# First mixture of experts: results scattered to their tokens' rows, a deeper fetch, and routing work moved between engines

## The chip, the core and the metric

One Trainium2 chip, one core of it. The metric is device time in microseconds (us) for one execution of the whole program, lower is better. The figure of a kernel is the median of its timed runs. The rows below come from one profiled execution.

## What is computed

The program is two transformer-like layers on 4096 tokens (B = 4, a 32 x 32 grid) of C = 192 float32 channels: attention, a mixture of 8 experts, attention, then a second block with its own attention, feed-forward and mixture of 4. The change touches the first mixture alone:

```python
logits = jnp.einsum('btd,ed->bte', x, gate_w)            # x: normed tokens, 8 experts
probs = jax.nn.softmax(logits, axis=-1)
selected_probs, selected_idx = jax.lax.top_k(probs, 2)
selected_probs = selected_probs / (jnp.sum(selected_probs, axis=-1, keepdims=True) + 1e-08)
a = jnp.einsum('btd,edh->bteh', x, gate_bank)            # h = 384
u = jnp.einsum('btd,edh->bteh', x, up_bank)
h = jax.nn.silu(a) * u
y_all = jnp.einsum('bteh,ehd->bted', h, down_bank)
y = sum over the 2 selected experts of y_all * selected_probs
```

The result y is added to the residual.

## The kernel before, in words

`routed_experts` computes only the two chosen experts of each token. Each engine has an instruction list of its own in one block, and semaphores written by hand order them. Its stages are these.

**Norm and transposes.** VectorE (DVE) normalises 32 tiles of 128 tokens into `rows` (L1904; shown as y). TensorE (PE) transposes them in 8 chunks of 512 tokens (L1729, L1730), ScalarE (ACT) copies each chunk out of PSUM into `room` (L1834; shown as xt). SyncE (SP) stores the normed rows to the DRAM tensor `xn` (normed_rows). Beside this the expert weights are loaded in 8 blocks by SP (`load_weights`, four raw buffers), and split into a float16 high part (ACT, `split_high`, L1824, L1825) and a low part (DVE, `split_low`, L1912, L1916). DVE has six of the eight low splits in its list ahead of the routing.

**Logits.** After each chunk of transposes PE makes the logits of the chunk before (`logit`, L1718): the 128 tokens of a tile are the weights and the 8 columns of `gw` move, so a chunk has 4 tiles x 2 halves of C, and each float32 product shows as two records.

**Routing.** DVE takes maximum, softmax, top 2 (L1927 to L1951), PE counts and ranks (L1740 to L1745), and DVE computes for each of the 2 x 4096 (token, choice) pairs a slot in a list that is sorted by expert and padded to blocks of 256 rows: 39 blocks, 78 groups of 128. To invert the list, one-hot matrices are built: `hi_hot` (L1976), `by_place` (L1980), `lo_hot` (L1981) by DVE and `by_pick` (L1683) by GpSimd (POOL); PE multiplies them (L1754, L1758) and DVE makes from the product `ids`, the pair held by each slot, and `take`, the token row to fetch. Between, DVE computes which expert owns a block (L1985 to L1990) and makes the last two low splits.

**Blocks.** For each of 39 blocks POOL fetches 256 rows of `xn` by two indirect DMAs (`fetch`, L1693), up to AHEAD = 3 blocks ahead; PE transposes them, makes gate and up products (L1782 to L1786) and the down products (L1799); ACT and DVE do silu, product and splits; ACT writes the result into `done` (L1862), two blocks behind; SP stores it to `yd` (expert_rows) in the order of the slots (L1668).

**Return.** When all 39 stores are in DRAM, POOL gathers the rows of every token tile with 64 indirect DMAs (L1705), 32 into `rows` and 32 into `wide` (vt); DVE, chunk by chunk of 512 tokens, adds them into the residual with their gate values (L2039, 8 of 128 x 192) and takes the statistics for the next norm (L2044, 4). Then the block ends, SP clears the mixture's semaphores (40 of them), and the next layer's norm begins (L123).

Of the kernel before, what the change touches and what calls it, by code (L numbers as in the profile page):

```python
# [24 lines left out]
T = B * L  # L25
# [61 lines left out]
def linker(engine, sem):  # L87

    count = [0]

    def link(ins):
        count[0] += 1
        ins.then_inc(sem, 1)
        engine.wait_ge(sem, count[0])

    return link

# [1450 lines left out]
def routed_experts(nc, name, res, rows, room, wide, stats, eps, ident, a, scratch, sent, experts, mt, w_gate, gate_bank,  # L1548
# [12 lines left out]
    AHEAD = 3  # L1561
# [6 lines left out]
    with Pool(nc, name) as m:  # L1568
# [6 lines left out]
        gw = [m.sb("gw0", experts), m.sb("gw1", experts, parts=C1)]  # L1575
# [14 lines left out]
        take, give = m.sb("take", SLOTS, U32), m.sb("give", PAIR, U32)  # L1590
# [10 lines left out]
        fetched = [room[1][:, at + u * 2 * C:at + (u + 1) * 2 * C] for u in range(AHEAD)]  # L1601
        done = [rows[:, at + u * 2 * C:at + (u + 1) * 2 * C] for u in range(AHEAD)]
# [9 lines left out]
        logits, ranks, counts, lists = banks[4:8]  # L1612
# [6 lines left out]
        s_turn, s_f32, s_lg = m.sem("turn"), m.sem("f32"), m.sem("logits")  # L1619
# [4 lines left out]
        s_sent = [m.sem(f"sent{r}") for r in range(AHEAD)]  # L1624
        s_add, s_bn = m.sem("add"), m.sem("bn")
        s_fetch, s_back = sent["fetch"], sent["back"]
# [10 lines left out]
        with nc.Block() as block:  # L1637
            @block.sync
            def _(sp):
# [25 lines left out]
                for b in range(BLOCKS):  # L1665
                    u = b % AHEAD
                    sp.wait_ge(s_y, b + 1)
                    sp.dma_start(yd[b * SPAN:(b + 1) * SPAN, :].rearrange("(j p) f -> p j f", p=P),  # L1668
                                 done[u].rearrange("p (j f) -> p j f", j=2)).then_inc(s_sent[u], 16)
                for r in range(AHEAD):  # L1670
                    sp.wait_ge(s_sent[r], 16 * len(range(r, BLOCKS, AHEAD)))

            @block.gpsimd
            def _(pool):
                for i, t in enumerate(bl):
                    pool.memset(t[C1:P, :], 0.0).then_inc(s_pad, 1)
                    pool.wait_ge(s_pad, i + 1)
                pool.memset(ones[:, :], 1.0).then_inc(s_pad, 1)

                pool.wait_ge(s_const, 48)  # L1680
                pool.wait_ge(s_xn, 16 * (T // CHUNK))
# [27 lines left out]

            @block.tensor  # L1710
            def _(pe):
# [11 lines left out]
                for n in range(T // CHUNK):  # L1723
# [8 lines left out]
                    if n:  # L1732
                        logit(n - 1)
# [84 lines left out]
            def _(act):  # L1818
# [11 lines left out]
                for n in range(T // CHUNK):  # L1830
# [4 lines left out]
                    if n % 2:  # L1835
                        split_high(n // 2)
# [413 lines left out]
```

## Time and profile before

| | us |
|---|---|
| median of 3 runs | 3374.49 |
| lowest and highest | 3373.45, 3380.55 |
| the profiled execution, its own time | 3370.78 |
| its span | 3368.9 |
| share of the span: PE, DVE, ACT, POOL busy | 82%, 72%, 55%, 13% |

The first mixture lies between about 797 and 1204 us of the span. In the rows below a time line gives start and duration in us, the engine, the source line, output and inputs by their names, a count, and in brackets how long the engine had been idle and what ended that. A q behind an engine's name is its queue of DMA issues.

### The profile page before, as it was taken

The page shows a single profiled execution, that of the slowest core. Times are in us where ns is not written, and L with a number is a line of the kernel's source. Part 1 is how long each engine was busy: PE and PEld are TensorE (multiplying, and loading weights), DVE is VectorE, ACT ScalarE, POOL GpSimd, SP SyncE. Part 2 cuts the span into 40 slices and gives each one's busy share as a digit, 9 for nine tenths or more (in the row PEclk, how much of TensorE's full clock was granted, in tenths as well). Part 3 has the DMA queues.
Part 4 walks back from the last instruction along what each step waited for, and adds up shares of the span by engine and source line. Part 5 has one row for each costly group of instructions (what it writes and reads, how often), then busy time and mean ns, then how long its engine had stood idle before and what let it go on. Part 6 is the DMA issues. An engine that isn't in the chain of part 4 may idle for free. (4 is left out here: it accounts for less than half of the span.)

```text
span 3368.9 us, 62705 instructions
## 1 busy us (share of the span) xinstructions
PE 2764.8 (82%) x18708; PEld 1277.7 (38%) x18708; DVE 2414.6 (72%) x4597; ACT 1860.7 (55%) x2592; POOL 435.2 (13%) x513
## 2 busy tenths in 40 slices
PE   5948999997499239589999956199999959599999
PEld 3612222226499126222222234022222236366666
DVE  6458999974766354579999955589999835465665
ACT  4416777773255124167777736067777736465554
POOL 0010111111333510101111110201111100000000
PEclk9759999996699667599999977599999979699999
DMA  2555776664122214567766701101111110200000
GB/s 64 169 125 114 151 148 142 148 126 143 33 78 76 70 31 146 134 110 150 149 146 149 145 22 50 57 28 52 48 48 49 48 32 1 55 22 5 9 5 14
DMA packets 202070, 277.27 MB, mean 82 GB/s; under 512 B 54302, under 2 KB 93454, under 8 KB 201930
## 3 DMA queue, kind: packets, MB, share of 16 engines
q1 hardware_dynamic: 162346, 211.32, 27.1%
q0 software_dynamic: 19920, 31.57, 4.0%
q10 hardware_dynamic: 19664, 32.60, 3.3%
q8 instruction: 77, 1.26, 0.2%
q14 instruction: 63, 0.52, 0.1%
HBM read 196.93 MB, written 77.46 MB: 81 GB/s over the span
## 5 line engine op out<-in xcount | busy, mean ns | idle before, releaser
L750 DVE TENSOR_REDUCE c1att_mx<-c1att_m 128x1 f32<-128x512 f32 x768 | 493.4, 685 | 35.7 <-PE c1att_m L688 30.6
L750 DVE TENSOR_REDUCE c0att_mx<-c0att_m 128x1 f32<-128x512 f32 x768 | 493.4, 685 | 32.5 <-PE c0att_m L688 27.2
L750 DVE TENSOR_REDUCE f1att_mx<-f1att_m 128x1 f32<-128x512 f32 x768 | 493.3, 685 | 26.5 <-PE f1att_m L688 21.8
L996 ACT ACTIVATE c1att_p<-c1att_s 128x1024 f32<-128x1024 f32 x384 | 373.9, 1020 | 152.0 <-PE c1att_s L703 151.9
L996 ACT ACTIVATE c0att_p<-c0att_s 128x1024 f32<-128x1024 f32 x384 | 373.9, 1020 | 148.8 <-PE c0att_s L703 148.7
L996 ACT ACTIVATE f1att_p<-f1att_s 128x1024 f32<-128x1024 f32 x384 | 373.9, 1020 | 143.8 <-PE f1att_s L703 142.8
L1426 ACT ACTIVATE moe_h<-moe_u,moe_bu 128x512 f32<-128x512 f32 x192 | 136.5, 711 | 175.6 <-PE moe_u L1343 93.9
L688 PE MATMUL f1att_m<-f1att_km,f1att_qm 16*128 16x512 f16 x768 | 155.7, 401 | 88.6 <-DVE f1att_ka L959 52.9
L716 PE MATMUL f1att_o<-f1att_p,f1att_vs 128*32 128x512 f32 x1536 | 206.2, 609 | 0.6 <-ACT f1att_p L996 0.6
L716 PE MATMUL c0att_o<-c0att_p,c0att_vs 128*32 128x512 f32 x1536 | 206.2, 609 | 0.6 <-ACT c0att_p L996 0.6
L716 PE MATMUL c1att_o<-c1att_p,c1att_vs 128*32 128x512 f32 x1536 | 206.1, 609 | 0.6 <-ACT c1att_p L996 0.6
L688 PE MATMUL c1att_m<-c1att_km,c1att_qm 64*128 64x512 f16 x768 | 156.2, 402 | 58.0 <-DVE c1att_mx L750 35.0
L688 PE MATMUL c0att_m<-c0att_km,c0att_qm 64*128 64x512 f16 x768 | 156.3, 403 | 57.7 <-DVE c0att_mx L750 34.8
L703 PE MATMUL f1att_s<-f1att_qa,f1att_ka 113*128 113x512 f16 x768 | 202.7, 385 | 0.8 <-ACT f1att_p L996 0.4
L1356 PE MATMUL moe_y<-moe_dh,xt 128*128 128x192 f16 x1536 | 195.1, 246 | 0.0
L1463 DVE TENSOR_TENSOR xt<-moe_h,xt 128x512 f16<-128x512 f32 x192 | 131.3, 691 | 86.3 <-ACT xt L1428 85.3
L1356 PE MATMUL moe_y<-moe_dl,xt 128*128 128x192 f16 x768 | 188.9, 246 | 0.0
L688 PEld LDWEIGHTS f1att_m<-f1att_km,f1att_qm 16*128 16x128 f16 x768 | 37.3, 92 | 322.6 <-DVE f1att_mx L750 264.3
L688 PEld LDWEIGHTS c1att_m<-c1att_km,c1att_qm 64*128 64x128 f16 x768 | 37.8, 93 | 292.3 <-DVE c1att_mx L750 262.4
L688 PEld LDWEIGHTS c0att_m<-c0att_km,c0att_qm 64*128 64x128 f16 x768 | 37.8, 93 | 291.7 <-DVE c0att_mx L750 262.2
L703 PE MATMUL c1att_s<-xt,c1att_ka 113*128 113x512 f16 x512 | 135.7, 387 | 7.6 <-DMA xt<-c1att_mrow 7.1
L1356 PEld LDWEIGHTS moe_y<-moe_dh,xt 128*128 128x128 f16 x1536 | 139.0, 98 | 3.7
(608 smaller groups left out, 5430.8 us busy)
## 6 DMA issues: line engine op xcount, KB each, us to landing
xt<-rel_parts SPq DMA_DIRECT2D x256, 128.0 KB, 5.0
xt<-qk_parts SPq DMA_DIRECT2D x192, 128.0 KB, 4.4
y<-rel_parts SPq DMA_DIRECT2D x128, 128.0 KB, 5.6
y<-qk_parts SPq DMA_DIRECT2D x96, 128.0 KB, 5.1
c0att_qm<-rel_parts SPq DMA_DIRECT2D x144, 64.0 KB, 2.1
c1att_qm<-rel_parts SPq DMA_DIRECT2D x144, 64.0 KB, 2.1
expert_rows<-y SPq DMA_DIRECT2D x39, 192.0 KB, 2.0
o_sums<-c0att_o ACTq DMA_DIRECT2D x24, 256.0 KB, 4.3
```

Of the source, the lines that this page charges most:

```text
L688: ins = pe.matmul(bank[:, :], qm[v][rows, q0:q0 + P], km[v][rows, c * CHUNK:(c + 1) * CHUNK], start=True, stop=True)
L703: ins = pe.matmul(sps[h][:, c * CHUNK:(c + 1) * CHUNK], ka[u][0:R_END, kcol], qa[u][0:R_END, queries(h, version, c * CHUNK, CHUNK)], start ...
L716: ins = pe.matmul(ops[row:row + 32, :], vs[u][:, (h * KT + kt) * 32:(h * KT + kt + 1) * 32], pr[h][kt % 2][:, c * CHUNK:(c + 1) * CHUNK], ...
L750: dve.tensor_reduce(mx[:, n:n + 1], bank[:, :], AX.X, ALU.max).then_inc(s_mx, 1)
L996: act.activation(pr[h][kt % 2][:, :], sps[h][:, :], ACT.Exp).then_inc(s_e, 1)
L1356: ins = pe.matmul(yps[q % 2][t // 2][:, (t % 2) * C:(t % 2 + 1) * C], hidden[q % 2][:, x], down[:, w], start=k == 0 and i == 0, stop=k == ...
L1426: act.activation(h32[:, i % 2 * CHUNK:(i % 2 + 1) * CHUNK], bank[:, :], ACT.Gelu, bias=bias, scale=1.0 / W_SCALE).then_inc(s_h32, 1)
L1463: dve.tensor_tensor(hl[q % 2][:, cols], h32[:, i * CHUNK:(i + 1) * CHUNK], hh[q % 2][:, cols], ALU.subtract).then_inc(s_hl, 1)
```

## The change

- **Return.** `send(b)` on POOL writes each block's 256 result rows by two indirect DMAs straight to row "choice x 4096 + token" of `yd`; the places are `give` (now from `ids`, one for each slot; empty slots are out of bounds and skipped). When all are there, SP reads `yd` back in order with 16 plain DMAs. The 39 stores by SP and the 64 gathers by POOL are gone.
- **Fetch.** Rows are fetched 6 blocks ahead, results kept in 3 buffers. POOL's list: six fetches, then `send(b)` and `fetch(b + 6)` in turn.
- **Logits.** `gw` is padded to 32 columns (two memsets by POOL ahead of its others, and SP waits for them before its first load) and is now the weights; 512 tokens move. Four chunks use the four 32-column tiles of PE side by side, twice. ACT copies the product out, PE transposes it back, DVE copies it from PSUM in 8 pieces. The splits of blocks 2 and 3 by ACT come after the last logits instead of among the chunks.
- **One-hot products.** `by_pick` is made by DVE; its order is `hi_hot`, `lo_hot`, `by_place`, `by_pick`.
- `s_back` (8 semaphores) and two for the logits are now among those cleared at the end, three fewer `s_sent`: 47.

```diff
-    AHEAD = 3
+    AHEAD, KEPT = 6, 3
...
-        gw = [m.sb("gw0", experts), m.sb("gw1", experts, parts=C1)]
+        gw = [m.sb("gw0", 32), m.sb("gw1", 32, parts=C1)]
...
-        take, give = m.sb("take", SLOTS, U32), m.sb("give", PAIR, U32)
+        take, give = m.sb("take", SLOTS, U32), m.sb("give", SLOTS, U32)
...
             def _(sp):
...
+                sp.wait_ge(s_pad, 2)
                 for t, src in zip(gw, (w_gate[0:C0, :], w_gate[C0:C, :])):
-                    sp.dma_start(t[:, :], src).then_inc(s_gw, 16)
+                    sp.dma_start(t[:, 0:experts], src).then_inc(s_gw, 16)
...
-                for b in range(BLOCKS):
-                    u = b % AHEAD
-                    sp.wait_ge(s_y, b + 1)
-                    sp.dma_start(yd[b * SPAN:(b + 1) * SPAN, :].rearrange("(j p) f -> p j f", p=P),
-                                 done[u].rearrange("p (j f) -> p j f", j=2)).then_inc(s_sent[u], 16)
-                for r in range(AHEAD):
-                    sp.wait_ge(s_sent[r], 16 * len(range(r, BLOCKS, AHEAD)))
+                for r in range(KEPT):
+                    sp.wait_ge(s_sent[r], 32 * len(range(r, BLOCKS, KEPT)))
+                for n in range(T // CHUNK):
+                    for k, tile in enumerate((rows, wide)):
+                        src = yd[k * T + n * CHUNK:k * T + (n + 1) * CHUNK, :]
+                        sp.dma_start(tile[:, n * 4 * C:(n + 1) * 4 * C].rearrange("p (t f) -> p t f", t=4),
+                                     src.rearrange("(t p) f -> p t f", p=P)).then_inc(s_back[n], 16)
...
             def _(pool):
+                for t in gw:
+                    pool.memset(t[:, :], 0.0).then_inc(s_pad, 1)
...
-                pool.wait_ge(s_hot, 2)
-                pool.tensor_tensor(by_pick.rearrange("p (k s) -> p k s", s=SLOTS),
-                                   hi_hot.rearrange("p (k s) -> p k s", s=SLOTS),
-                                   table[:, COUNT:COUNT + PAIR].unsqueeze(2).broadcast_to([P, PAIR, SLOTS]),
-                                   ALU.mult).then_inc(s_picks, 1)
...
+                def send(b):
+                    u = b % KEPT
+                    pool.wait_ge(s_y, b + 1)
+                    for j in range(2):
+                        pool.indirect_dma_start(
+                            yd[:, :], bass.IndirectOffsetOnAxis(give[:, 2 * b + j:2 * b + j + 1], 0),
+                            done[u][:, j * C:(j + 1) * C], None,
+                            bounds_check=2 * T - 1, oob_is_err=False).then_inc(s_sent[u], 16)
+
+                pool.wait_ge(s_xn, 16 * (T // CHUNK))
                 pool.wait_ge(s_idx, 2)
+                for b in range(AHEAD):
+                    fetch(b)
                 for b in range(BLOCKS):
-                    fetch(b)
-                for r in range(AHEAD):
-                    pool.wait_ge(s_sent[r], 16 * len(range(r, BLOCKS, AHEAD)))
-                for n in range(T // CHUNK):
-                    for k, tile in enumerate((rows, wide)):
-                        for t in range(4 * n, 4 * n + 4):
-                            pool.indirect_dma_start(
-                                tile[:, t * C:(t + 1) * C], None, yd[:, :],
-                                bass.IndirectOffsetOnAxis(give[:, k * TILES + t:k * TILES + t + 1], 0)
-                                ).then_inc(s_back[n], 16)
+                    send(b)
+                    if b + AHEAD < BLOCKS:
+                        fetch(b + AHEAD)
...
-                def logit(n):
-                    pe.wait_ge(s_f32, 2 * n + 2)
-                    for j in range(4):
-                        t = 4 * n + j
-                        for k, c in enumerate((C0, C1)):
-                            ins = pe.matmul(logits[:, t * experts:(t + 1) * experts], room[k][0:c, t * P:(t + 1) * P],
-                                            gw[k][0:c, :], start=k == 0, stop=k == 1)
+                def logits(i):
+                    pe.wait_ge(s_f32, 8 * i + 8)
+                    for k, c in enumerate((C0, C1)):
+                        for j in range(4):
+                            ins = pe.matmul(banks[4 + i][32 * j:32 * j + 32, :], gw[k][0:c, :],
+                                            room[k][0:c, (4 * i + j) * CHUNK:(4 * i + j + 1) * CHUNK],
+                                            start=k == 0, stop=k == 1)
                     ins.then_inc(s_lg, 1)
+
+                def logits_back(i):
+                    pe.wait_ge(s_lgc, i + 1)
+                    for t in range(4):
+                        ins = pe.transpose(banks[6 + i][:, t * P:(t + 1) * P], raw_lg[i][:, t * P:(t + 1) * P], ident)
+                    ins.then_inc(s_lgt, 1)
...
-                    if n:
-                        logit(n - 1)
-                logit(T // CHUNK - 1)
+                    if n == 4:
+                        logits(0)
+                    if n == 6:
+                        logits_back(0)
+                logits(1)
+                logits_back(1)
...
-                    if n % 2:
-                        split_high(n // 2)
-                for blk in range(T // CHUNK // 2, experts - 2):
+                    if n % 4 == 1:
+                        split_high(n // 4)
+                    if n == 4:
+                        logits_out(0)
+                logits_out(1)
+                for blk in range(2, experts - 2):
                     split_high(blk)
...
-                    if b >= AHEAD:
-                        act.wait_ge(s_sent[u], 16 * (b // AHEAD))
+                    if b >= KEPT:
+                        act.wait_ge(s_sent[u], 32 * (b // KEPT))
...
+                for i in range(2):
+                    dve.wait_ge(s_lgt, i + 1)
+                    to = key[:, i * 16 * experts:(i + 1) * 16 * experts].rearrange("p (j t e) -> p t j e", j=4, e=experts)
+                    source = banks[6 + i][:, :].rearrange("p (t j e) -> p t j e", t=4, j=4)
+                    for t in range(4):
+                        inc(dve.tensor_copy(to[:, t], source[:, t, :, 0:experts]))
+                link(dve.memset(low_one[:, 0:1], 0.0))
...
+                dve.wait_ge(s_hot, 2)
+                dve.tensor_scalar(by_place, hi_hot, place[:, :], None, ALU.mult).then_inc(s_hot, 1)
+                dve.wait_ge(s_xn, 16 * (T // CHUNK))
+                dve.tensor_tensor(by_pick.rearrange("p (k s) -> p k s", s=SLOTS),
+                                  hi_hot.rearrange("p (k s) -> p k s", s=SLOTS),
+                                  table[:, COUNT:COUNT + PAIR].unsqueeze(2).broadcast_to([P, PAIR, SLOTS]),
+                                  ALU.mult).then_inc(s_picks, 1)
...
-                dve.tensor_copy(give[:, :], slot[:, :]).then_inc(s_idx, 1)
+                link(dve.tensor_scalar(empty[:, :], ids[:, :], 0.0, 1.0e5, ALU.is_lt, ALU.mult))
+                dve.tensor_tensor(give[:, :], ids[:, :], empty[:, :], ALU.add).then_inc(s_idx, 1)
...
-                    dve.wait_ge(s_back[n], 128)
+                    dve.wait_ge(s_back[n], 32)
```

## Rows read from the trace of the kernel before

**Rows 1.** The page's first line: the span.
```profile
span 3368.9 us, 62705 instructions
```

**Rows 2.** Busy time by stretch: PE, PEld, DVE, ACT, POOL, then clock, DMA share, GB/s.
```profile
920.00:960.00 40.00, 40.00 (x404) 37.30 (x403) 24.63 (x64) 23.70 (x72) 14.36 (x16) 1.00 0.29 78
1130.00:1206.00 76.00, 0.00 (x0) 0.00 (x0) 29.00 (x89) 0.00 (x0) 51.95 (x53) 0.50 0.26 70
2924.60:2932.30 7.70, 7.61 (x33) 0.96 (x34) 0.00 (x0) 0.62 (x2) 0.00 (x0) 0.50 0.66 174
```

**Rows 3.** DVE in order of time, the return: first chunk, last chunk, next layer.
```profile
1127.36 1.40 DVE L2039 SCALAR_TENSOR_TENSOR x<-y,f_top,x 128x192 f32<-128x192 f32 x4 [16.68 <-DMA vt<-expert_rows,f_give]
...
1199.50 1.41 DVE L2039 SCALAR_TENSOR_TENSOR x<-y,f_top,x 128x192 f32<-128x192 f32 x4 [6.36 <-DMA vt<-expert_rows,f_give]
...
1202.38 1.14 DVE L2044 BATCH_NORM_STATS2 stats<-x 128x6 f32<-128x192 f32 x4
1206.99 0.21 DVE L123 TENSOR_TENSOR c1ln_mean<-stats 128x32 f32<-128x32 f32 x1 [3.47 <-PEq L68]
```

**Rows 4.** POOL in order of time: the last of the 64 gathers.
```profile
1196.84 0.94 POOL L1705 DMA_INDIRECT vt<-expert_rows,f_give  x1 [0.30 <-issue]
```

**Rows 5.** ACT in order of time: results of blocks 0, 36 and 38.
```profile
921.79 0.48 ACT L1862 ACTIVATE y<-f_bank 128x384 f32<-128x384 f32 x1
...
1108.43 0.48 ACT L1862 ACTIVATE y<-f_bank 128x384 f32<-128x384 f32 x1
...
1112.58 0.49 ACT L1862 ACTIVATE y<-f_bank 128x384 f32<-128x384 f32 x1 [1.67 <-PE f_bank L1799]
```

**Rows 6.** Program start: SP's loads of x, 768 KB each, and DVE's first work on them.
```profile
0.99 4.92 SPq L2124 DMA_DIRECT2D x<-in_x  x4
```
```profile
5.96 2.18 DVE L2119 BATCH_NORM_STATS2 stats<-x 128x6 f32<-128x192 f32 x8 [5.96 <-DMA x<-in_x]
```

**Rows 7.** Groups of POOL instructions: busy us, mean ns, idle before them and releasers.
```profile
L1693 POOL DMA_INDIRECT xt<-normed_rows,f_take x78 | 73.8, 947 | 120.4 <-PE f_bank L1769 99.8 <-issue 12.8 <-DVE f_give L2001 7.8
```

**Rows 8.** PE in order of time: the last logits here, and the second mixture's.
```profile
841.19 8.28 PE L1718 MATMUL f_bank<-f_gw,xt 128*128 128x8 f32 x32
```
```profile
2924.69 7.52 PE L1102 MATMUL moe_y<-xt,moe_gw 128*32 128x512 f32 x32 [16.86 <-DMA moe_b<-in_exp_b]
2932.14 1.97 PE L1109 MATMUL moe_y<-ident,moe_h 128*128 128x128 f32 x8
```

**Rows 9.** ACT and SP in order of time: high splits of blocks 4 and 5, block 5's load.
```profile
844.62 0.51 ACT L1824 ACTIVATE f_ah<-vt 128x384 f16<-128x384 f32 x1
...
848.50 0.67 ACT L1825 ACTIVATE f_dh<-vt 128x576 f16<-128x576 f32 x1
```
```profile
834.56 0.59 SPq L1648 DMA_DIRECT2D vt<-in_f_down  x1
```

**Rows 10.** DVE in order of time: first routing step, then one-hots to the index list.
```profile
852.39 0.41 DVE L1927 TENSOR_REDUCE f_one<-f_bank 128x32 f32<-128x256 f32 x1
...
869.52 5.36 DVE L1976 TENSOR_TENSOR xt<-f_table,f_slothi 128x4992 f16<-128x4992 f32 x1
...
876.36 8.68 DVE L1981 TENSOR_TENSOR vt<-f_table,f_slotlo 128x8192 f16<-128x8192 f32 x1
884.96 8.83 DVE L1985 TENSOR_TENSOR f_past<-f_table,f_ends 128x312 f32<-128x312 f32 x1
...
894.43 0.55 DVE L1912 SCALAR_TENSOR_TENSOR f_al<-f_raw,f_ah 128x384 f16<-128x384 f32 x1
...
899.51 0.22 DVE L1995 TENSOR_SCALAR f_ids<-f_bank 128x78 f32<-128x78 f32 x1
```

**Rows 11.** POOL in order of time: its first memsets, `by_pick`, the first fetch.
```profile
797.39 5.36 POOL L1676 MEMSET f_bl<- 64x3072 f16 x2 [10.60 <-POOLq L68]
...
876.62 16.83 POOL L1683 TENSOR_TENSOR y<-xt,f_table 128x4992 f16<-128x4992 f16 x1 [73.60 <-DVE xt L1980]
901.28 1.07 POOL L1693 DMA_INDIRECT xt<-normed_rows,f_take  x1 [7.83 <-DVE f_give L2001]
```

More of the change, by code:

```diff
@@ L96, in linker, with chain, inc, link @@
     return link
+def chain(engine, sem):
+    count = [0]
+    def inc(ins):
+        count[0] += 1
+        ins.then_inc(sem, 1)
+    def link(ins):
+        inc(ins)
+        engine.wait_ge(sem, count[0])
+    return link, inc
 def layer_norm(nc, name, src, eps, stats, turned_to, ident, gain=None, shift=None, parts=None, inner=None, direct=False):
@@ L1600, in routed_experts @@
         at = (PAIR * SLOTS + 1) // 2
-        fetched = [room[1][:, at + u * 2 * C:at + (u + 1) * 2 * C] for u in range(AHEAD)]
-        done = [rows[:, at + u * 2 * C:at + (u + 1) * 2 * C] for u in range(AHEAD)]
+        fetched = [rows[:, at + u * 2 * C:at + (u + 1) * 2 * C] for u in range(AHEAD)]
+        done = [room[1][:, at + u * 2 * C:at + (u + 1) * 2 * C] for u in range(KEPT)]
         at = PAIR * P
@@ L1611, in routed_experts @@
         t0, t1 = banks[0:2], banks[2:4]
-        logits, ranks, counts, lists = banks[4:8]
+        ranks, counts, lists = banks[4:7]
+        raw_lg = [wide[:, 2 * RAW + i * CHUNK:2 * RAW + (i + 1) * CHUNK] for i in range(2)]
         turned, units, sums = banks[0:2], banks[2:6], banks[6:8]
@@ L1618, in routed_experts @@
         s_chain, s_std, s_norm, s_xn = m.sem("chain"), m.sem("std"), m.sem("norm"), m.sem("xn")
-        s_turn, s_f32, s_lg = m.sem("turn"), m.sem("f32"), m.sem("logits")
+        s_turn, s_f32, s_lg, s_lgc, s_lgt = (m.sem(n) for n in ("turn", "f32", "logits", "lcopy", "lturned"))
         s_exp, s_route, s_chosen, s_rank = m.sem("exp"), m.sem("route"), m.sem("chosen"), m.sem("rank")
@@ L1623, in routed_experts @@
         s_up, s_s, s_h32, s_hh, s_hl, s_down, s_y = (m.sem(n) for n in ("up", "s", "h32", "hh", "hl", "down", "y"))
-        s_sent = [m.sem(f"sent{r}") for r in range(AHEAD)]
+        s_back = [m.sem(f"back{n}") for n in range(T // CHUNK)]
         s_add, s_bn = m.sem("add"), m.sem("bn")
-        s_fetch, s_back = sent["fetch"], sent["back"]
+        s_fetch, s_sent = sent["fetch"], sent["sent"]
         def cube(t):
@@ L1826, in split_high, with logits_out @@
                                    scale=W_SCALE).then_inc(s_wh, 1)
+                def logits_out(i):
+                    act.wait_ge(s_lg, i + 1)
+                    act.activation(raw_lg[i], banks[4 + i][:, :], ACT.Copy).then_inc(s_lgc, 1)
                 act.wait_ge(s_chain, 6)
@@ L1884, in _ @@
             def _(dve):
-                link = linker(dve, s_chain)
+                link, inc = chain(dve, s_chain)
                 half_of = stats[:, :].rearrange("p (t s) -> p s t", s=6)
@@ L1978, in _ @@
                                   slot_hi[:, :].unsqueeze(2).broadcast_to([P, PAIR, SLOTS]), ALU.is_equal).then_inc(s_hot, 1)
-                dve.wait_ge(s_hot, 1)
-                dve.tensor_scalar(by_place, hi_hot, place[:, :], None, ALU.mult).then_inc(s_hot, 1)
                 dve.tensor_tensor(lo_hot.rearrange("p (k s) -> p k s", s=P),
@@ L2106, in build @@
         by_pool = {"past": 0} | {k: ctx.enter_context(nc.semaphore(f"{k}_by_pool")) for k in ("z", "rzst", "numinv")}
-        sent = {k: [ctx.enter_context(nc.semaphore(f"{k}{r}_by_pool")) for r in range(n)] for k, n in (("fetch", 3), ("back", T // CHUNK))}
+        sent = {k: [ctx.enter_context(nc.semaphore(f"{k}{r}_by_pool")) for r in range(n)] for k, n in (("fetch", 6), ("sent", 3))}
         with Pool(nc, "start") as m:
```

18 lines of the change are left out of this document (7 added, 11 removed).

## The prediction

> **What bounds the kernel now.** The change touches one stage, so I read the page for the span [rows 1] and then only that stage, first as busy time by stretch, then each engine in order of time. Three regimes are to be seen. In the block loop PE is busy 40.00 us of 40.00 at full clock [rows 2]: nothing in the loop that is not PE can save time, it can only cost some. In the return PE is at 0.00, DVE is busy 29 of 76 us and the DMA engines are at 0.26 of their time, while POOL is at work throughout [rows 2]: POOL's descriptor work sets the pace. DVE waited 16.68 us for its first chunk and 6.36 us before its last [rows 3], and the gathers follow each other at 0.94 + 0.30 us, started by nothing but the end of the one before [rows 4]. Between norm and loop there is a serial chain: the last logits, the routing, the one-hots, the index list, the first fetch [rows 8, 10, 11].
>
> **Return, the large term.** Before: the last result is in SBUF at 1112.58 + 0.49 = 1113.07 [rows 5], the last statistics end at 1202.38 + 1.14 = 1203.52 [rows 3]; 90.45 us. After, in the times of this trace: POOL must still send blocks 36, 37 and 38, the first and last of whose results come at 1108.43 + 0.48 = 1108.91 and 1113.07 [rows 5], closer together than two sends a block would be. A scatter does not occur before. Nearest is the gather: 1.25 us from one to the next [rows 4], of which 0.947 us work [rows 7]. I take 1.25 us. Six in a row from 1109.1 put the last issue at 1115.35. From issue to the released reader the last gather took 1199.50 - 1196.84 = 2.66 us [rows 3, 4], so the rows are in DRAM at 1118.0. SP then reads 768 KB for each chunk of 512 tokens, as much as one load of x at the start has; the first of these took 5.96 - 0.99 = 4.97 us until DVE began, and four were issued in 4.92 us [rows 6]. DVE begins at 1123.0. A chunk is 1202.38 + 1.14 - 1199.50 = 4.02 us of DVE work [rows 3]; the x loads were issued at 1.23 us for 768 KB, so even two DMAs for each chunk at that price, 2.5 us, stay ahead, and DVE sets the pace: 8 x 4.02 and 0.05 between them is 32.5, end 1155.5. Gain 48.0 us. If the first chunk lands after 4 or 8 us it is 49 or 45.
>
> **The loop.** Removed: 39 issues on SP, which costs nothing, as SP has nothing else there. Added: 78 scatters in POOL's list, in front of each later fetch. The deeper fetch gives nothing, since PE never idled between 920 and 960 [rows 2] with three ahead. It is cover: with six ahead, a fetch queued behind a send that waits for its result is still in time. POOL's sum: the first send can start at 922.27 [rows 5], and behind it are 66 fetches and 78 sends. With 1.25 us each they end no earlier than 922.27 + 180 = 1102.3, and the last result is at 1113.07; so they fit, with 11 us to spare in 191. That slack is thin: a scatter of 1.42 us uses it up, and each further 0.1 us costs 7.8 us at the end. ACT waits for the send of three blocks ago before it writes `done`: nothing until POOL is that far behind. The memory traffic is the same as before.
>
> **One-hots.** From `hi_hot` to the first fetch it is now 901.28 - 869.52 = 31.76 us [rows 10, 11]. The chain ran through POOL: `by_pick` ends at 876.62 + 16.83 = 893.45 [rows 11], then PE's second half, then DVE's index work at 899.51. DVE was held too: `past`, 312 columns, took 8.83 us and ended as POOL did [rows 10], where 4992 columns took 5.36. After, on DVE alone: `hi_hot` and `by_place` 6.84 (876.36 - 869.52), `lo_hot` 8.60, `by_pick` unknown, `past` some 0.5, its two followers 0.6, the two low splits 899.51 - 894.43 = 5.08, the index work to the first fetch 1.77, `give` in two steps +0.27. For `by_pick` the same number of columns and the same table as operand as in `hi_hot` say 5.36; bounds are 1.5 (the whole difference 6.84 - 5.36, for `by_place`) and 8.8. The sum is 29.0; gain 2.7 us (6.5 to -0.7). PE's first half lies under `by_pick`, the second under the splits, which last longer.
>
> **Logits.** Old: 16 records in 4.1 us, after each chunk (8.28 us for the last 32 [rows 8]), 33 us in all with PE the pace, the last at 849.5. New, from the second mixture, which has this very form: 32 records in 7.52 us and the transposes back in 1.97, at the low clock 0.50 [rows 2, 8]. So PE gets some 24 us back. But DVE and ACT take over: DVE's list has six low splits ahead of the routing, ACT now has splits 2 to 5 behind `logits_out(1)`. With transposes at some 1.7 us for a chunk and ACT's two copies and splits between, I get the last logits at about 830, and ACT's four splits at (848.50 + 0.57 - 844.62) / 2 = 2.2 us each [rows 9] from 830.6. Block 5's weights are issued at 834.56 [rows 9], at the end of one unbroken series on SP, and land by 834.56 + 4.97 = 839.5 at the latest by the bound of [rows 6]. So high part 5 ends at 841.7, low part 5 (5.08 / 2 = 2.54) at 844.25, the eight small copies and the memset 1.2 more (0.9 to 2.2: 0.24 each is the pitch of a small DVE instruction that waits [rows 3], and these don't wait), and the two new memsets in front of everything 0.3. Routing starts at 845.75 instead of 852.39: gain 6.6 us (3 to 8.5). The routing itself doesn't change.
>
> **Block end.** 40 semaphores are cleared within 3.47 us [rows 3], at most 0.09 each; seven more, 0.5 us.
>
> **Sum.** -48.0 - 2.7 - 6.6 + 0.5 = -56.8 us. The profiled execution took 3370.78 us, 3.7 below the median 3374.49, so it would give 3314; on the median 3317.7. I predict 3318.
>
> **A rule that speaks against it.** The stores leave SP for POOL, and POOL's work can be held up by DVE: `past` and `by_pick` above hindered each other [rows 10, 11]. In the loop, though, fetches cost 0.947 us in the mean beside a DVE that is busy 24.63 of 40 us [rows 2, 7]. The Trainium skill, "SBUF — State Buffer", section "Who interferes with whom", says that DMAs issued by GpSimd starve while VectorE runs an operation that takes both ports, and advises SP or ACT as issuer. By that rule each scatter might wait for a DVE instruction; by the rows none does.
>
> **Rivals.**
> - *POOL becomes the bound of the loop.* For: a slack of 0.17 us for each scatter; bounds checking and DRAM as the target have no row. Against: 0.947 on all 78 fetches. If a scatter waited for one DVE instruction of some 0.4 us (1.67), POOL ends at 922.27 + 82.5 + 130.3 = 1135, not 1116.6: +18.5, 3336.
> - *The front gives nothing*: weights land later or the splits are the true chain. For: six low splits stand before the routing. Against: block 5 is issued by 835. Time 3374.5 - 47.5 = 3327.
> - *The read back is not faster than the gathers*, 10.4 us for a chunk (1.3 x 8), because it is the rows of 768 bytes and not the descriptors that cost. For: as many rows. Against: DMA share 0.26 then [rows 2]. Gain some 9 + 9: 3356.
> - *Slower*: a scatter costs 2.2 us or more, 1.75 times a gather. Then POOL ends at 922.27 + 82.5 + 171.6 = 1176, +60, and PE waits in the loop for its fetches: 3377 and more. It decides from 2.17 us on.
>
> **Chances.** The forecast 0.66 (own range 3309 to 3325), POOL as bound 0.17 (3320 to 3345), front nothing 0.08, slow read back 0.05, slower 0.04. The range takes in the first three: 3305 to 3336. A measurement of this kernel tells about 0.2%, 7 us, from no change. Faster 0.95, same 0.01, slower 0.04.
>
> **What would show it.** The last result to the next norm in about 42 + 4 us; scatters at 1.25 us pitch; PE without idle time in the loop; DVE's return chunks back to back; routing 6 to 7 us earlier, bounded by low part 5; `by_pick` near 5.4 us and `past` near 0.5. I would be wrong if the scatters' pitch is over 1.42, if DVE waits before each chunk of the return, or if the clock falls in the loop.

## The result, and the profile after

The kernel after took 3402.57 us (median of four runs, 3399.93 to 3406.23), the kernel before, timed beside it, 3375.21 us; the ratio is 1.0079 [1.0062, 1.0097]. So the change came out slower by 0.8%, where the prediction said 3318 us. Later the same file, unchanged, was loaded anew four times in three other jobs and took 3315 to 3317 us each time, 1.6% faster than the kernel before. (A job is one stay on a chip, in which several kernels are timed in turn, the kernel before always among them.) Both numbers have to be explained, and only one of them is.

First the profile of that first timing, which I call the first job. The page's span, and its granted clock in 40 slices of the span, in tenths of full speed:

```profile
span 3402.8 us, 62616 instructions
...
PEclk9759999997688858579999987599999979699999
```

Busy time by stretch: the start of the loop, the rest of the loop, the return (columns as in [rows 2]):

```profile
905.00:920.00 15.00, 12.46 (x103) 9.88 (x101) 6.70 (x18) 6.07 (x21) 4.06 (x5) 0.93 0.13 36
920.00:1185.00 265.00, 223.68 (x1872) 184.21 (x1871) 111.68 (x288) 102.46 (x322) 139.58 (x138) 0.88 0.18 50
1190.00:1230.00 40.00, 0.00 (x0) 0.00 (x0) 28.80 (x89) 0.17 (x1) 3.64 (x4) 0.55 0.52 158
```

In the loop PE is busy 84% of the time, where it was busy 40.00 of 40 us [rows 2], and its granted clock is 0.88 in place of 1.00. Half of the 83 us that the loop lost, as worked out below, is PE's idle time, 41.3 us between 920 and 1185; the rest is time in which PE counts as busy and gets on more slowly, its matmuls at the lower clock above all. The groups of waits in the loop (us in total, times, the longest) name hardly any engine and no DMA for PE:

```profile
DVE vt L2066 <- ACT vt L1904: 115.3, 50, 8.1
POOL expert_rows L1713 <- ACT xt L1895: 100.2, 26, 11.3
...
PEld f_bank L1809 <- issue: 13.5, 13, 1.4
PEld f_bank L1812 <- issue: 12.7, 13, 1.3
PEld f_bank L1825 <- issue: 9.8, 11, 1.9
```

"issue" means that the profile shows nothing for which the engine waited. The named waits of PE in this stretch come to 5.0 us, six waits for DVE's `xt`. POOL waits for results (100.2 us), so it is not the bound: it waits for the others. PE in order of time, inside such a gap:

```profile
958.27 0.27 PE L1810 MATMUL f_bank<-vt,f_ah 128*128 128x256 f16 x1
958.54 0.27 PE L1811 MATMUL f_bank<-vt,f_bh 128*128 128x256 f16 x1
959.28 0.27 PE L1812 MATMUL f_bank<-vt,f_bl 128*128 128x256 f16 x1 [0.47 <-issue]
960.01 0.27 PE L1808 MATMUL f_bank<-vt,f_ah 128*128 128x256 f16 x1 [0.46 <-issue]
960.72 0.27 PE L1809 MATMUL f_bank<-vt,f_al 128*128 128x256 f16 x1 [0.44 <-issue]
960.83 0.27 PE L1810 MATMUL f_bank<-vt,f_ah 128*128 128x256 f16 x1
962.14 0.38 PE L1811 MATMUL f_bank<-vt,f_bh 128*128 128x256 f16 x1 [1.04 <-issue]
962.32 0.42 PE L1812 MATMUL f_bank<-vt,f_bl 128*128 128x256 f16 x1
```

The profile shows nothing that they wait for; they start every 0.72 us, or after twice that, instead of every 0.11 us. The matmul at 962.14 takes 0.38 us and the next 0.42, in place of 0.27: the clock has gone from 2.4 to 1.2 GHz behind the gap, as the clock column (the third from the right) says of the gap and of the time behind it:

```profile
958.50:961.00 2.50, 1.14 (x6) 0.23 (x4) 0.00 (x0) 0.00 (x0) 1.99 (x2) 1.00 0.23 79
962.20:964.00 1.80, 1.28 (x5) 0.50 (x6) 0.00 (x0) 0.14 (x1) 0.04 (x1) 0.50 0.21 55
```

POOL meanwhile issues at its usual pitch:

```profile
957.34 1.03 POOL L1713 DMA_INDIRECT expert_rows<-xt,f_give  x1 [0.30 <-issue]
958.68 1.00 POOL L1713 DMA_INDIRECT expert_rows<-xt,f_give  x1 [0.30 <-issue]
959.99 0.98 POOL L1705 DMA_INDIRECT y<-normed_rows,f_take  x1 [0.30 <-issue]
```

Such gaps come in a pattern that for most of the loop repeats every 22.7 us, three blocks: when POOL issues eight DMAs in one go, PE stalls for some 5 us in the second half of them and 1.2 us beyond; four in one go leave one short gap of 0.2 to 1.6 us or none, and the longer of these are put down to DVE's `xt`. Three blocks take 22.7 us in place of 15.6. PE's gaps without a named wait, those over 0.2 us, all start 4.8 us or more behind the first DMA of such a go and end within 2 us of its last.

Outside the loop the stage is near the forecast. DVE and ACT in order of time, from the last result to the next layer:

```profile
1189.68 0.49 ACT L1895 ACTIVATE xt<-f_bank 128x384 f32<-128x384 f32 x1 [1.93 <-issue]
...
1200.34 1.41 DVE L2082 SCALAR_TENSOR_TENSOR x<-y,f_top,x 128x192 f32<-128x192 f32 x4 [12.51 <-DMA vt<-expert_rows]
...
1231.11 1.14 DVE L2087 BATCH_NORM_STATS2 stats<-x 128x6 f32<-128x192 f32 x4
1235.62 0.22 DVE L138 TENSOR_TENSOR c1ln_mean<-stats 128x32 f32<-128x32 f32 x1 [3.37 <-PEq L68]
```

The return is 1190.17 to 1232.25, 42.1 us, where it was 90.45 (worked out from [rows 3, 5]). POOL's first memset starts at 801.63 (797.39 in [rows 11]), the routing at 848.70, the first fetch at 895.40 and the last result ends at 1190.17. Against [rows 3, 5, 10, 11] the stage's parts are: up to the routing -7.9 us, routing to first fetch -2.2, loop +83.0, return -48.4, block end -0.1; in sum +24.4. The loop's 294.8 us (211.8 before) hold the whole miss.

### The profile page after: what moved, and what is told of

Its sections match the earlier page's. It is cut to its first block and busy times, and to the rows that moved or that the text cites. A ratio compares the mean times of both kernels' runs of the same rounds, so it can differ in the third digit from the quotient of the medians.

```text
span 3402.8 us, 62616 instructions
## 1 busy us (share of the span) xinstructions
PE 2782.0 (82%) x18620; PEld 1259.2 (37%) x18620; DVE 2413.9 (71%) x4608; ACT 1857.8 (55%) x2594; POOL 439.1 (13%) x528
## 5 line engine op out<-in xcount | busy, mean ns | idle before, releaser
L2066 DVE SCALAR_TENSOR_TENSOR vt<-f_bank,vt 128x256 f32<-128x256 f32 x117 | 49.7, 425 | 161.3 <-ACT vt L1904 127.0
```

What stands on the lines that cost most here:

```text
L2066: dve.scalar_tensor_tensor(out=h32[n % 2], in0=units[n % UNITS][:, SPAN:2 * SPAN], scalar=1.0 / W_SCALE, in1=s_buf[n % 2], op0=ALU.mult, o ...
```

## The experiments

I took the sends for the cause, since the stalls came when POOL issued without a break. The first four kernels ran together, in another job (the kernel before: 3369.68 us there). The first two leave out that the results reach their tokens' rows.

**plain_stores**, no sends: SP stores results in slot order and nothing gathers them.

```
-                for b in range(BLOCKS):
-                    send(b)
-                    if b + AHEAD < BLOCKS:
-                        fetch(b + AHEAD)
+                for b in range(AHEAD, BLOCKS):
+                    fetch(b)
...
+                    sp.dma_start(yd[b * SPAN:(b + 1) * SPAN, :].rearrange("(j p) f -> p j f", p=P),
+                                 done[u].rearrange("p (j f) -> p j f", j=2)).then_inc(s_sent[u], 16)
```

> Everything of the change but the scatters: SP stores each block's result in slot order as the kernel before did, POOL only fetches (six ahead), and the return reads the first 8192 slots in order, so the rows added are not those of their tokens. Theory 1 (POOL's indirect DMAs, four for a block and nearly without a gap, hold up PE's instruction stream): no gaps in PE's stream, loop back to 5.2 us a block, time about 3318. Theory 2 (the scatters' writes to DRAM): the same here. Theory 3 (the six-deep fetch or the new places of the buffers in SBUF): the loop stays at about 7.5 us a block, time about 3400.

Measured: 3309.85 us, ratio 0.982 [0.980, 0.984], no stall: as theories 1 and 2 had it.

**twins**, two more gathers in each pair of sends' place, SP storing:

```
+                        pool.indirect_dma_start(
+                            dump[u][:, j * C:(j + 1) * C], None, xn[:, :],
+                            bass.IndirectOffsetOnAxis(take[:, 2 * b + j:2 * b + j + 1], 0)).then_inc(s_twin[u], 16)
```

> As plain_stores, and POOL makes two further gathers for each block into unused SBUF, at the place in its list where the scatters stood. Same number of indirect DMAs as the changed kernel, but no scatter. Theory 1: the same gaps in PE's stream (5 us long, from some 6 us after the start of a run of eight), about 7.5 us a block, time 3395 to 3405. Theory 2: no gaps, about 3320. Theory 3: as plain_stores.

Measured: 3320.04 us, 0.985 [0.9831, 0.987], as theory 2 had it. POOL issued 122 gathers in a row with no more than 0.5 us between two (0.44 ahead of each block's added pair, 0.30 otherwise), and PE did not stall.

**ahead4**, `AHEAD, KEPT = 4, 3`:

> The changed kernel with rows fetched four blocks ahead and not six; POOL's opening run is eight fetches and not twelve. Theories 1 and 2: the same time within 5 us (3395 to 3405), since each block still has four indirect DMAs. Theory 3, if the depth is the cause: faster by tens of us.

Measured: 3617.82 us, 1.0734 [1.0712, 1.0755], which none of the three theories had. The waits between 940 and 1170 us are of another kind than the first job's:

```profile
POOL expert_rows L1713 <- ACT xt L1895: 149.2, 17, 9.3
PEld f_bank L1794 <- DMA y<-normed_rows,f_take: 107.5, 17, 7.2
PE f_bank L1794 <- DMA y<-normed_rows,f_take: 103.7, 17, 6.9
```

PE's transposes wait for a fetch, once a block, 6 us. The fetch of block b + 4 stands in POOL's list behind the two sends of block b, which wait for b's result, and PE needs it in block b + 3. So depth is needed for this order of the list, for a reason that has nothing to do with the first job's stalls.

**front_only**, the new logits and one-hots with the loop and the return of before (AHEAD = 3, SP's stores, POOL's 64 gathers):

> The new logits, the one-hot products all by VectorE and the padded gate weights, but loop and return as before. My working for the front alone: 9.3 us gained less nothing at the end of the block, so 3366 against 3375 (ratio 0.9972); the trace of the changed kernel has the first fetch 10.1 us earlier after the start of the stage, which would give 3365. Rival: the front's gain is lost again in the loop, ratio 1.000.

Measured: 3362.91 us, 0.9978 [0.9969, 0.9988], or -7.4 us (-10.5 to -4.0). In its trace the stage, from POOL's first memset to the next layer's first work, is 10.0 us shorter.

By then I believed in the sends (theory 2). The next four asked which property of them it was (the kernel before: 3370.82 us).

**no_check** gives each empty slot a spare row behind the 8192 (three more lines for DVE, not shown), so that the bound falls away:

```
-                            done[u][:, j * C:(j + 1) * C], None,
-                            bounds_check=2 * T - 1, oob_is_err=False).then_inc(s_sent[u], 16)
+                            done[u][:, j * C:(j + 1) * C], None).then_inc(s_sent[u], 16)
```

> The kernel after, with the sends' test of the row number taken away: every empty slot gets a spare row of its own behind the 8,192 (two more small operations by VectorE ahead of the loop), so that nothing has to be left out and no send carries a bound; the sent rows of tokens and their order are the same. Theory A (it is the bounds test: the two register moves of 0.58 us ahead of each pair of sends, and what the test does on GpSimd while TensorE issues in steps of 0.7 us): the stalls of 5 us in every third block go, the loop is 5.2 us a block again, some 3,312 to 3,322 us. Theory B (it is the sends themselves, DMAs by row numbers that write DRAM from SBUF): the pairs of moves go but TensorE stalls as before, 3,395 to 3,405 us.

**in_order** drops the bound too and sends each block's rows to neighbouring places, which are not their tokens':

```
+                link(dve.tensor_scalar(token[:, :], table[:, COUNT:COUNT + SLOTS], float(P), place[:, :], ALU.mult, ALU.add))
+                dve.tensor_scalar(give[:, :], token[:, :], -1.0, None, ALU.add).then_inc(s_idx, 1)
```

> As no_check, but the sends' row numbers are 128 s + p, the slots' own order, so that each send writes 128 rows side by side (its result is not the tokens': the return reads the first 8,192 slots). Theory B1 (sends write rows that lie all over DRAM, and that is what holds TensorE): 3,312 to 3,322 us if no_check is slow. Theory B2 (any send by row numbers): as no_check, within 0.3%. If no_check is fast this is fast too.

**twins_check** puts `bounds_check=T - 1, oob_is_err=False` on the two added gathers of twins:

> twins (rows stored in slot order by SyncE, two more gathers of each block in the sends' place) with the bounds test on those two gathers, so that GpSimd makes the same two register moves ahead of them as the kernel after makes ahead of its sends. Theory A (bounds test): TensorE stalls in steps of 0.7 us again and the time is above 3,380 us. Theory B (sends): as twins, 3,320 us within 0.3%.

**sp_late** adds `sp.wait_ge(s_y, BLOCKS)` ahead of SP's waits on the sends:

> The kernel after, but SyncE waits for the last block's result before it looks at the sends' semaphores; in the kernel after it stands on the first of them through the whole loop. Theory C (TensorE's slow issue comes from an engine that stands waiting on a semaphore that GpSimd's DMAs raise): the stalls go, 3,312 to 3,322 us. Theories A and B: no change, 3,400 us within 0.3%.

Measured: no_check 3317.92 us (0.9846 [0.9829, 0.9864]), in_order 3315.44, twins_check 3318.41, sp_late 3316.62. All fast, none with a stall. Each theory has a run against it: sp_late keeps the bound and is fast, and so is twins_check (against A, the bounds test); no_check, in_order and sp_late keep the sends and are fast (against B); no_check keeps SP's early wait and is fast (against C). What the four share is that they are not the first job. That was the theory to test next, and it should have been the first.

**after_again**, the unchanged file, and **sp_twice**, which repeats SP's last wait so that its code is one instruction longer:

```
+                sp.wait_ge(s_xn, 16 * (T // CHUNK))
                 for r in range(KEPT):
```

> The kernel after, unchanged, run again. Theory C (SyncE's early wait on the sends' semaphores holds TensorE back): 3,400 us within 0.3%, with the stalls of 0.7 us a step in every third block, as in its first run. Theory D (the stalls are no property of the program: no_check left SyncE's wait as it was, sp_late left the sends' bounds test, twins_check put the test on gathers, and none of the three stalled, so what they have in common is only that they are not that build in that run): 3,312 to 3,322 us and no stall.

> The kernel after with one more SyncE wait, on the normed rows' semaphore that it has just waited for, so that it is met at once: SyncE still stands on the sends' semaphores through the loop, and only SyncE's code is one instruction longer, as in sp_late. Theory C: 3,400 us within 0.3%. Theory D, or a fourth (E: where the code lies decides, and one instruction moves it): 3,312 to 3,322 us. after_again tells D from E: by E it is slow, by D fast.

Measured: after_again 3316.01 us (four runs, 3307.99 to 3319.02), 0.9831 [0.981, 0.9853]; sp_twice 3313.61. The windows of after_again, start of the loop, loop, return:

```profile
905.00:920.00 15.00, 15.00 (x150) 13.89 (x148) 9.87 (x26) 8.91 (x29) 6.48 (x7) 1.00 0.16 45
920.00:1100.00 180.00, 180.00 (x1805) 167.83 (x1803) 107.65 (x278) 102.23 (x310) 133.91 (x135) 1.00 0.27 72
1105.00:1145.00 40.00, 0.00 (x0) 0.00 (x0) 29.40 (x91) 0.37 (x1) 3.55 (x4) 0.54 0.52 158
```

PE is busy 180.00 of 180 us at clock 1.00, with the same instructions, while POOL issues 101 DMAs without a break. The stalls are no fixed property of the program.

**after_third** and **ahead5** (`AHEAD, KEPT = 5, 3`):

> The kernel after, unchanged, a third time. Theory D (the stalls belong to the one execution job in which it was first timed): 3,316 us within 0.3%, ratio 0.982 to 0.985, no step of 0.7 us. If the stalls come back here, they belong to the program and some condition that differs from job to job, and the time is 3,400 us within 0.3%.

> The kernel after with AHEAD = 5 (ahead4 took 3,618 us, TensorE stood 6 us a block on a fetch that GpSimd had queued behind two sends). In ahead4's trace a fetch lands some 6.5 us after the result that lets its block's sends start, and the transposes that need it come one block of 5.2 us too early; one block more of depth gives 5.2 us. First theory (the queue behind the sends decides, and five blocks are enough): 3,316 us within 0.5%. Second theory (a block more is not quite enough, TensorE waits about 1 us a block): about 3,390 us. The prediction's own words (depth is cover and gives nothing) hold between five and six if the first is right.

Measured: after_third 3316.46 us, 0.9841 [0.9828, 0.9854], no stall. ahead5 3345.33 us, 0.9928 [0.991, 0.9946], between the two theories. Its waits from 920 to 1120:

```profile
POOL expert_rows L1713 <- ACT xt L1895: 28.4, 21, 2.8
PEld f_bank L1794 <- DMA y<-normed_rows,f_take: 26.0, 26, 2.5
PE f_bank L1794 <- DMA y<-normed_rows,f_take: 19.8, 24, 2.3
```

26 waits for a fetch of 1.0 us each: the same mechanism as in ahead4, nearly hidden.

**ahead8** (`AHEAD, KEPT = 8, 3`), **after_fourth** and **after_fifth** (unchanged):

> The kernel after with AHEAD = 8. From 4 to 5 to 6 blocks of depth the time fell 3,618, 3,345, 3,316 us. First theory (at six no fetch is waited for: TensorE is busy 40.00 of 40 us in the rerun of the kernel after): 3,316 us within 0.3%. Second (GpSimd's four DMAs a block fill its 5.2 us and it falls behind late in the loop, which more lead would hide): some 3 to 6 us less.

> The kernel after, unchanged, a fourth time. 3,316 us within 0.3% and no steps of 0.7 us if the first job's stalls stay alone; 3,400 us if they are a state that the program's loads fall into now and then.

> The same file once more, loaded anew. As after_fourth: 3,316 us within 0.3% without the stalls, or 3,400 us if they are a state of some loads.

Measured: ahead8 3319.21 us (0.9847 [0.983, 0.9864]), after_fourth 3316.74, after_fifth 3315.47. Two blocks more of depth give nothing, and the stalls don't come back.

**load_half** and **load_full** add useless traffic beside the loop, 512 and 2048 rows for each block:

```
+                for b in range(BLOCKS):
+                    sp.wait_ge(s_y, b + 1)
+                    sp.dma_start(scratch["spill"][b * SPILL:(b + 1) * SPILL, :], xn[0:SPILL, :]).then_inc(s_spill, 16)
```

> The kernel after, with useless traffic beside its loop: at each block's result SyncE starts a copy of 512 normed rows (393 KB) from DRAM to DRAM, which in some 5.2 us adds as much again as the loop's own 74 GB/s of reads. Theory F (the first job's stalls came from other traffic to memory or on the DMA engines in that job, and TensorE's instructions wait with the rest): steps of 0.7 us in TensorE's issue, with no wait for a fetch, and some 3,330 to 3,400 us. Against it (the traffic is not what did it): 3,316 to 3,325 us, or, if longer, TensorE waiting for fetches, which the first job's profile doesn't show.

> As load_half with 2,048 rows (1.57 MB) a block, more than the DMA engines can move in 5.2 us. TensorE will wait for late fetches here under either theory; what is asked is whether its trace also has the steps of 0.7 us in the issue of matmuls between waits (theory F) or only waits on fetches (against it). Time 3,450 to 3,800 us.

Measured: 3404.28 us (1.0085 [1.0065, 1.0105]) and 3411.33 us (1.0102 [1.0073, 1.0131]), both with the steps of 0.7 us. That looks like theory F. But load_full was expected at 3450 us or more with waits for fetches, and its trace has two such waits between 920 and 1185, 3.1 us in all; and the kernel before took 3375.88 us in this job. PE of load_full in order of time:

```profile
907.94 0.27 PE L1814 MATMUL f_bank<-vt,f_al 128*128 128x256 f16 x1
908.44 0.27 PE L1815 MATMUL f_bank<-vt,f_ah 128*128 128x256 f16 x1 [0.22 <-issue]
909.82 0.27 PE L1816 MATMUL f_bank<-vt,f_bh 128*128 128x256 f16 x1 [1.12 <-issue]
910.54 0.28 PE L1817 MATMUL f_bank<-vt,f_bl 128*128 128x256 f16 x1 [0.45 <-issue]
911.24 0.39 PE L1813 MATMUL f_bank<-vt,f_ah 128*128 128x256 f16 x1 [0.42 <-issue]
```

and SP's queue:

```profile
919.88 8.27 SPq L1685 DMA_DIRECT2D spilled_rows<-normed_rows  x2
```

The first stall, 907.9 to 911.2, lies ahead of the first copy at 919.88, so the copies can't have made it; nor have the sends, the first of which is issued at 920.6. It lies where the first job had one too (909.6 to 912.3), at the end of POOL's first twelve fetches. And 0.79 of the DMA engines' time and 259 GB/s in the loop (0.18 and 50 in the first job) left PE about as busy, 218.07 us of 265 (223.68). The columns are as in [rows 2]:

```profile
920.00:1185.00 265.00, 218.07 (x1846) 180.14 (x1844) 110.18 (x284) 101.62 (x317) 138.98 (x138) 0.90 0.79 259
```

From the first fetch to the last result the loop takes 293.5 us in load_half and 298.0 in load_full, against 294.8 in the first job. What load_full's time has more comes at the return too, where DVE first waits 21.25 us for its rows (12.75 in load_half).

**load_full_again**, the same file:

> load_full once more, the same file. Its job and the first job had one thing in common: the kernel before took 3,375.2 and 3,375.9 us in them, and 3,369.5 to 3,371.3 us in the five jobs without stalls. Theory G (the chip or its state decides, not the traffic: 23 MB and 58 MB moved in the same 230 us gave stalls of one kind, and the first of them came at 908 us, before the first copy): where the kernel before takes some 3,370 us this one shows no step of 0.7 us, and takes 3,316 to 3,340 us; where it takes some 3,375 us, 3,411 us and the stalls. Theory F (the traffic makes them): 3,411 us within 0.4% and the steps, whatever the kernel before takes.

Measured: 3409.8 us, 1.010 [1.0083, 1.0116], stalls again, the first from 904.9 to 907.7, and the first copy is issued at 916.4. Its loop takes 300.4 us. The kernel before took 3377.85 us. By its own condition this run is of the slower sort of job, where theories F and G say the same, so it does not tell them apart.

The jobs side by side, with the number of the chip that each ran on:

| job | chip | before, us | kernels of the change in it | TensorE's steps of 0.7 us |
|---|---|---|---|---|
| first | not on record | 3375.21 | after 3402.6 | yes |
| 2 | 14 | 3369.68 | plain_stores, twins, front_only; ahead4 waits for fetches | no |
| 3 | 14 | 3370.82 | no_check, in_order, twins_check, sp_late 3315 to 3318 | no |
| 4 | 15 | 3371.28 | after_again 3316.0, sp_twice 3313.6 | no |
| 5 | 14 | 3369.52 | after_third 3316.5, ahead5 | no |
| 6 | 13 | 3370.03 | after_fourth 3316.7, after_fifth 3315.5, ahead8 | no |
| 7 | 10 | 3375.88 | load_half 3404.3, load_full 3411.3 | yes |
| 8 | 6 | 3377.85 | load_full_again 3409.8 | yes |

The chips separate the jobs as well as anything does: none of the five jobs on chips 13, 14 and 15 stalled, and the two on chips 10 and 6 did. No chip is known to have had both, and the unchanged file is not known to have run on chip 10 or 6.

## Why the prediction was wrong

**The step that failed** is "The loop": removed and added work at nothing, and PE as the only bound. In the first job the loop took 83.0 us more. It did not fail by the condition that the prediction named. A send costs 1.01 to 1.04 us in the mean (1.31 to 1.34 from one to the next), under the 1.42 us from which POOL would become the bound, and POOL waited 100 us for results. (The prediction took 1.25 us. Its 11 us of slack over 78 sends allow 1.39 and not 1.42, which changes nothing here.) What replaced it: PE's own issue in steps of 0.72 us, each gap followed by the lower clock. "The clock falls in the loop" was on the list of what would make the forecast wrong; the rivals had no mechanism for it.

**What is shown of the cause.** The stalls are not fixed in the program: four later loads of the unchanged file show PE without idle time, two of them with four and five runs. They are no wait for a fetch: ahead4 and ahead5 show what that looks like. The kernel before has at most a little of them in the three stalled jobs: its medians lie within 0.3% of each other in all eight, so the condition of the job alone doesn't cost it what it costs the kernel after. The first stall of a loop needs neither a send nor a copy, as both come later.

**What stays open.** What the three stalled jobs had in common, and what in the kernel after answers to it and in the kernel before doesn't. The chip is a rival that no run tests: a property of chips 10 and 6 fits the table as well as a state that comes and goes. The kernel before was slower in just these three, by 4 to 8 us; that is a correlation over eight jobs, not a cause. Nor is it shown that the kernel before is free of stalls there. Its one trace has none: its first twelve fetches too follow without a break, from 901.28 to 916.24, and PE stays busy behind them, where the four stalled traces have their first stall.

```profile
915.00:920.00 5.00, 5.00 (x52) 4.68 (x51) 3.11 (x8) 2.50 (x8) 1.69 (x2) 1.00 0.17 43
```

But that execution took 3370.78 us, less than any of the first job's four timed runs (3373.45 and more) and as much as the median in jobs without stalls, so it doesn't stand for a stalled job. That the added traffic has no part in the later stalls of jobs 7 and 8 is likely, since four times as much moved the time by 0.2%, but it is not shown: the unchanged file ran in no second job of the slower sort. Also, plain_stores, twins, no_check, in_order, twins_check and sp_late all ran in jobs in which nothing stalled. Their speed says nothing on whether sends, bounds or POOL's long runs matter in a stalling job; the reading "it is the sends", which I drew from the first two, was wrong to draw. The next step would be one job on chip 10 or 6, and one on chip 14, each with the unchanged file, the kernel before and the file without its sends, all traced.

**The rest by its steps, in after_again**, where nothing stalled. The rows that answer to [rows 3, 5, 10, 11] follow, engine by engine in order of time. POOL at the stage's start:

```profile
800.02 0.17 POOL L1693 MEMSET f_gw<- 128x32 f32 x2 [10.50 <-POOLq L68]
```

ACT and DVE, block 5's first high split and last low one; DVE, the first routing step and the one-hots:

```profile
841.58 0.52 ACT L1850 ACTIVATE f_ah<-vt 128x384 f16<-128x384 f32 x1 [2.01 <-DMA vt<-in_f_down]
...
845.83 0.74 DVE L1949 SCALAR_TENSOR_TENSOR f_dl<-vt,f_dh 128x576 f16<-128x576 f32 x1
...
847.41 0.42 DVE L1965 TENSOR_REDUCE f_one<-f_key 128x32 f32<-128x256 f32 x1
...
864.13 5.36 DVE L2013 TENSOR_TENSOR xt<-f_table,f_slothi 128x4992 f16<-128x4992 f32 x1
869.40 8.68 DVE L2016 TENSOR_TENSOR vt<-f_table,f_slotlo 128x8192 f16<-128x8192 f32 x1
878.12 1.52 DVE L2020 TENSOR_SCALAR xt<-xt,f_place 128x4992 f16<-128x4992 f16 x1
879.56 5.35 DVE L2022 TENSOR_TENSOR y<-xt,f_table 128x4992 f16<-128x4992 f16 x1
884.82 0.48 DVE L2027 TENSOR_TENSOR f_past<-f_table,f_ends 128x312 f32<-128x312 f32 x1
```

POOL, the first fetch and the last send:

```profile
893.67 1.09 POOL L1705 DMA_INDIRECT y<-normed_rows,f_take  x1 [87.79 <-DVE f_give L2044]
...
1108.48 0.98 POOL L1713 DMA_INDIRECT expert_rows<-xt,f_give  x1 [0.30 <-issue]
```

ACT, the last result:

```profile
1104.88 0.49 ACT L1895 ACTIVATE xt<-f_bank 128x384 f32<-128x384 f32 x1 [1.63 <-PE f_bank L1825]
```

DVE, the return and the next layer's first work:

```profile
1115.08 1.40 DVE L2082 SCALAR_TENSOR_TENSOR x<-y,f_top,x 128x192 f32<-128x192 f32 x4 [12.06 <-DMA vt<-expert_rows]
...
1145.49 1.14 DVE L2087 BATCH_NORM_STATS2 stats<-x 128x6 f32<-128x192 f32 x4
1150.00 0.22 DVE L138 TENSOR_TENSOR c1ln_mean<-stats 128x32 f32<-128x32 f32 x1 [3.37 <-PEq L68]
```

- *Logits*, forecast -6.6: 847.41 - 800.02 = 47.39 us from POOL's first memset to the routing, 852.39 - 797.39 = 55.00 before; -7.6. The mechanism is the one forecast: block 5's weights land last, low part 5 ends at 846.57, 46.6 us into the stage (844.25 - 797.39 = 46.9 forecast), and the routing follows 0.84 us behind it (1.5 taken).
- *One-hots*, -2.7: 893.67 - 847.41 = 46.26 against 48.89 from routing to first fetch; -2.6. `by_pick` took 5.35 us (5.36 taken), `past` 0.48 (0.5).
- *Loop*, 0: 893.67 to 1105.37 is 211.7 us against 211.8.
- *Return*, -48.0: 1105.37 to 1146.63 is 41.3 us against 90.45; -49.2. The last send is issued 3.1 us behind the last result (2.3 taken), DVE begins 6.6 us after that (7.65 taken), then eight chunks back to back, 31.6 us (32.5 taken).
- *Block end*, +0.5: 3.37 us against 3.47; -0.1.

The sum is -59.6 us, forecast -56.8. The medians differ by 55.3. The traces of these two executions differ by 51.9 us in their spans: in after_again the stage begins 2.6 us later, and what follows it, which the change does not touch, took 5.1 us longer; over all traces that rest lies between 2161.5 and 2169.9 us. front_only gives the first two terms by themselves, -7.4 us by the timed runs and -10.5 by its trace. plain_stores shows what the sends still cost at the end: without them DVE begins 6.4 us after the last result, with them 9.7.

**Depth.** "The deeper fetch gives nothing ... It is cover" is right at six, and has a price now where it is missing: 29 us at five blocks, 301 us at four. The prediction did not say how many blocks the cover needs.

**The rule on who interferes with whom.** The prediction set the Trainium skill ("SBUF — State Buffer", section "Who interferes with whom": DMAs that GpSimd issues starve behind VectorE's two-port operations) against the fetches' 0.947 us. No such wait shows for the sends: 1012 ns in the mean in after_again and 1036 at most, in a loop where DVE is busy 107.65 of 180 us; 1042 ns in the mean and 1275 at most in the first job. But this is no test of the rule. DVE's instructions in the loop are of the kinds TENSOR_TENSOR and SCALAR_TENSOR_TENSOR alone, and the section names copies, casts and tensor_scalar as those that can take both ports.

## What to carry to other kernels

When the profile of a changed kernel shows a loss for which it names no wait ("issue"), run the same file again in another job, and note the chip, before changing anything: here six kernels were spent on a fault that was not even present in their jobs. An experiment that removes a suspect proves something only if the unchanged kernel, beside it in the same job, still shows the fault. And where a queue's order puts a fetch behind a send, count depth from the send's release to the fetch's reader: here six blocks hide it and five do not.

## What the runs showed of the hardware

- TensorE can issue its matmuls in steps of 0.72 us (0.11 us is usual), with no wait that a profile shows, in some jobs and not in others, with the same program: 3402.6 against 3316 us. Whether the chip or something else decides is open. The gaps bring the clock down as well, 0.88 in the mean in place of 1.00, so that matmuls take 0.42 us in place of 0.27.
- A send of 128 rows of 768 bytes by row numbers costs GpSimd 1.01 us (1.31 to 1.34 from one to the next), 0.04 more than a fetch of the same size; its bounds test costs nothing that the time shows (no_check 3317.9 us).
- The loop in its stalled state went on at nearly the same pace with the DMA engines at 0.79 of their time and 259 GB/s as at 0.18 and 50 GB/s: 298.0 against 294.8 us, in two different jobs. No run adds traffic where nothing stalls.
- VectorE's compare `past` of 128 x 312 took 8.83 us beside GpSimd's product `by_pick` and ended 0.34 us behind it [rows 10, 11]; with that product gone from GpSimd it took 0.48 us (after_again).
